# Cross-attention and FFN layer: the first batch's input transposes and first queries are issued ahead of the branch, and the start is reordered

## The reference

```python
def reference(...):                       # cut to what is computed
    q = layernorm(x) @ w_q;  k = ctx @ w_k;  v = ctx @ w_v          # 16 heads of 64
    attn = softmax(where(mask, -inf, q @ k.T / 8))
    x = x + (attn @ v) @ w_o
    w = int4_quantize(kernel)             # scale = max|kernel| / 7, round, clip, times scale
    h = layernorm(x)
    return x + h @ w + bias + (h @ a) @ b
```

## Time and profile before

| what | value |
|---|---|
| median of 3 runs | 540.42 us (539.54 to 540.65) |
| the profiled execution: time, span | 538.71 us, 536.9 us |
| mean granted TensorE clock in it | 0.958 |
| busy: PE, PEld, DVE, ACT, POOL | 468.2, 337.9, 423.2, 330.9, 400.3 us |
| busy in the first 30 us: PE, DVE, ACT, POOL | 7.30, 20.84, 17.29, 9.31 us |

### The profile page before, as it was taken

One profiled execution on the slowest core, in us unless ns is written; L12 is line 12 of the kernel. 1 busy time (PEld: TensorE's weight loads), 2 busy tenths in 40 slices (PEclk: granted clock), 3 DMA queues, 4 the chain that ended last, 5 costly groups with the idle time before them and its releaser, 6 DMA issues.

```text
span 536.9 us, 15609 instructions
## 1 busy us (share of the span) xinstructions
PE 468.2 (87%) x5939; PEld 337.9 (63%) x5939; DVE 423.2 (79%) x1138; ACT 330.9 (62%) x839; POOL 400.3 (75%) x658
## 2 busy tenths in 40 slices
PE   2239678998999899999999899989999999988874
PEld 0125365667766686667766776668666777666663
DVE  4945757988898888988898879888798878888762
ACT  4815456676667776676567666776667656666521
POOL 3364187888878787879878887878787787789941
PEclk9559979999999999999999999999999999999897
DMA  8310157668866788688767896688757786679950
GB/s 304 109 59 21 29 132 146 112 127 165 159 120 123 135 186 123 125 149 165 141 112 136 160 160 123 125 129 189 130 120 149 97 146 130 131 130 168 178 130 24
DMA packets 217953, 71.10 MB, mean 132 GB/s; under 512 B 202497, under 2 KB 216594, under 8 KB 217874
## 3 DMA queue, kind: packets, MB, share of 16 engines
q1 hardware_dynamic: 216528, 67.65, 64.9%
q0 software_dynamic: 768, 2.10, 1.2%
q10 hardware_dynamic: 578, 0.30, 0.2%
HBM read 15.50 MB, written 4.19 MB: 37 GB/s over the span
## 4 chain that ended last, share of the span: by engine, by line
PE 48%; DVE 27%; ACT 13%; POOL 5%; issue 4%; DMA 2%; POOLq 0%; DVEq 0%; ACTq 0%
PE ps_b L812 38%; DVE ps_a L703 6%; PE ps_a L874 6%; ACT arena L586 6%; DVE arena L696 4%; ACT arena L577 2%; PE ps_b L915 2%; DVE arena L652 2%; PE ps_b L891 2%; DVE arena L775 1%; DVE arena L707 1%; POOL arena L512 1%; DMA mask_u<-in_mask_1x1xSxS_bk_dram 1%; POOL arena L516 1%; ACT arena L593 1%
## 5 line engine op out<-in xcount | busy, mean ns | idle before, releaser
L812 PE MATMUL ps_b<-arena 128*128 128x65 f16 (+3 forms) x3456 | 346.3, 253 | 14.6 <-DVE arena L676 5.3
L812 PEld LDWEIGHTS ps_b<-arena 128*128 128x128 f16 x3456 | 234.2, 99 | 103.1 <-DVE arena L676 6.7
L586 ACT ACTIVATE arena<-ps_a,arena 128x160 f32<-128x160 f32 x512 | 159.4, 395 | 95.9 <-DVE arena L707 87.5
L516 POOL TENSOR_TENSOR arena<-arena 128x512 f16<-128x512 f32 x128 | 148.2, 1158 | 0.0
L512 POOL CAST arena<-arena 128x512 f16<-128x512 f32 x128 | 78.2, 611 | 74.7 <-ACT arena L586 74.7
L703 DVE TENSOR_REDUCE ps_a<-ps_a 128x4 f32<-128x640 f32 x128 | 105.4, 823 | 0.2
L874 PE MATMUL ps_a<-arena 64*128 64x160 f16 x1536 | 76.4, 233 | 14.5 <-ACT arena L586 11.2
L874 PEld LDWEIGHTS ps_a<-arena 64*128 64x128 f16 x1536 | 50.9, 95 | 39.2 <-issue 22.2
L891 PE MATMUL ps_b<-arena 128*128 128x65 f16 x512 | 71.7, 194 | 0.0
L696 DVE TENSOR_TENSOR arena<-ps_b,arena 128x512 f16<-128x512 f32 x64 | 43.7, 686 | 24.9 <-ACT arena L577 24.1
L775 DVE TENSOR_TENSOR arena<-ps_b,arena 128x256 f32<-128x256 f32 x128 | 54.3, 425 | 4.4
(11 more groups left out here) (122 smaller groups left out, 437.5 us busy)
## 6 DMA issues: line engine op xcount, KB each, us to landing
arena<-in_x_dram SPq DMA_DIRECT2D x8, 512.0 KB, 5.2
mask_u<-in_x_dram SPq DMA_DIRECT2D x32, 128.0 KB, 2.9
out_dram<-mask_u SPq DMA_DIRECT2D x32, 128.0 KB, 2.4
arena<-arena SPq DMA_TRANSPOSE x128, 3.8
arena<-in_L_xattn_w_k_dram SPq DMA_DIRECT2D x1, 1024.0 KB, 8.5
arena<-in_L_xattn_w_v_dram SPq DMA_DIRECT2D x1, 1024.0 KB, 10.5
arena<-in_L_xattn_w_q_dram SPq DMA_DIRECT2D x1, 1024.0 KB, 12.3
arena<-in_L_xattn_w_o_dram SPq DMA_DIRECT2D x1, 1024.0 KB, 14.2
```

What stands on the lines that cost most here:

```text
L516: nc.gpsimd.tensor_tensor(lo_main, main, hi_main, ALU.subtract)
L586: ins = nc.scalar.activation(probs[k % 2][:, h, :], p_scores[k % 2][:, h % 2, h // 2 * WINDOW:(h // 2 + 1) * WINDOW], ACT.Exp, bias=neg_ma ...
L812: mm = nc.tensor.matmul(dst, a, c, start=(first and at == 0), stop=(last and at == n - 1))
```

## The change

Names and order change; no instruction of the computation is dropped, and none is added except that some are issued at another place or in another form.

- The queries' weights are loaded and halved first (`W_ORDER`). POOL makes their low half ahead of the branch; that of the values moves behind it.
- Ahead of the branch TensorE also turns `xn` (`x0`, `x1`) and makes `q0`, `q1`, `q2`; ACT takes their high halves between its weight copies; DVE makes the low halves of `x0`, `x1` in the midst of its span chain. The low halves of `q0` to `q2` stand first behind the branch.
- The keys' scaled copy on ACT is gone: DVE makes the keys' low half in one instruction with the scaling (`scalar_tensor_tensor`) ahead of `q3`.
- The item order behind the branch is `q3 q4 q5 c q6 k0 k1 q7 k2 k3 v0 v1 r0 r1`. `maxima(0)` and `exps(0)` follow `k1`, the statistics follow `q7`, `keep` follows `k3`, `norm_apply` follows `v0`.
- The FFN weights are made in two parts, `ffn_grid` after `v0` and the rest after `r1`. The bias copy goes ahead of the branch, and the waits for FFN weights and output weights go to the first items that use them.

```diff
-        ALL_PROJ = [i for slot in PROJ for i in slot]
+        EARLY = ["x0", "x1", "q0", "q1", "q2"]
+        ALL_PROJ = EARLY + ["q3", "q4", "q5", "c", "q6", "k0", "k1", "q7", "k2", "k3", "v0", "v1", "r0", "r1"]
...
-        W_ORDER = (1, 2, 0, 3)
+        W_ORDER = (0, 1, 2, 3)
+        SCALED_ORDER = (0, 2, 3)
...
-            split_low(nc.gpsimd, 0)
+            split_low(nc.gpsimd, 2)
...
-            split_low(nc.vector, 1)
             for i, name in enumerate(ALL_PROJ):
+                if name in EARLY[0:DT]:
+                    continue
+                if name == "q3":
+                    dve.wait_ge(split_hi, 2)
+                    nc.vector.scalar_tensor_tensor(out=w_lo[1], in0=raw_w[1], scalar=WS, in1=w_hi[1], op0=ALU.mult,
+                                                   op1=ALU.subtract).then_inc(split_lo[1], 1)
                 item(start, i, name)
-                if name == "k3":
+                if name == "q7":
                     for t in range(ST):
                         norm_stats(t, 32)
                     norm_var()
-                if name == "q2":
+                if name == "v0":
+                    ffn_grid(dve)
+                if name == "k3":
...
-                if name == "q5":
+                if name == "k1":
                     maxima(0)
-                if name == "q7":
-                    ffn_weights(dve)
+            ffn_weights(dve)
...
-                if name == "q5":
+                if name == "k1":
                     scores(0)
-            pe.wait_ge(ffn_made, 1)
-            scores(1)
+                if name == "k2":
+                    pe.wait_ge(bias_copied, 1)
+                    scores(1)
             pe.wait_ge(keep_made, 1)
-            pe.wait_ge(split_lo[3], 1)
-            pe.wait_ge(ffn_split, 1)
...
-            split_low(nc.gpsimd, 2)
+            split_low(nc.gpsimd, 0)
             path(pool, fast_pool, general_pool)
...
+            high(0)
+            rescale(0)
+            for j in range(DT):
+                act.wait_ge(item_made, j + 1)
+                nc.scalar.activation(xT_hi[:, j, :], p_item[j][:, :], ACT.Copy).then_inc(item_hi, 1)
+            high(1)
+            high(2)
+            rescale(2)
+            for j in range(len(EARLY) - DT):
+                act.wait_ge(item_made, DT + j + 1)
+                nc.scalar.activation(f_q[0][:, 0, j, :], p_item[(DT + j) % LANES][:, :], ACT.Copy).then_inc(item_hi, 1)
+            high(3)
+            rescale(3)
             path(act, fast_act, general_act)
...
+            for j in range(DT):
+                dve.wait_ge(item_hi, j + 1)
+                nc.vector.tensor_tensor(xT_lo[:, j, :], p_item[j][:, :], xT_hi[:, j, :], ALU.subtract) \
+                    .then_inc(item_done, 1)
             link(nc.vector.tensor_tensor_reduce(out=scratch, in0=penalty, in1=key_left, scale=1.0, scalar=LOWEST,
                                                 op0=ALU.add, op1=ALU.max, accum_out=col(FIRST)))
...
+            dve.wait_ge(bias_made, 1)
+            nc.vector.tensor_copy(bias_all[:, :], p_bias[:, 0:D]).then_inc(bias_copied, 1)
             dve.wait_ge(ffn_max_spread, 1)
...
             nc.tensor.transpose(p_max_row, ffn_scale[:, 0:1], ident[:, :]).then_inc(ffn_max_turned, 1)
+
+            w_q_hi, w_q_lo = (w[0].rearrange("p (t n) -> p t n", t=DT) for w in (w_hi, w_lo))
+            pe.wait_ge(xn_made, ST)
+            for j in range(DT):
+                for t in range(ST):
+                    mm = nc.tensor.transpose(p_item[j][:, t * P:(t + 1) * P], xn[:, t, j * P:(j + 1) * P], ident[:, :])
+                mm.then_inc(item_made, 1)
+
+            pe.wait_ge(split_lo[0], 1)
+            pe.wait_ge(item_done, DT)
+            for j in range(len(EARLY) - DT):
...
             pe.wait_ge(ffn_max_row, 1)
```

More of the change, by code:

```diff
@@ L147, in xattn_ffn @@
         f_raw = Layout()
-        raw_w = [f_raw.take([DT * HD]) for _ in range(4)]
+        raw_q = f_raw.take([DT * HD])
+        f_raw.at = f.at // 2
+        raw_k, raw_v = f_raw.take([DT * HD]), f_raw.take([DT * HD])
         w_hi = [f.take([DT * HD], fp16) for _ in range(4)]
@@ L180, in xattn_ffn @@
         inv_sum = [f.take([GROUP]) for _ in range(2)]
+        f_raw.at = f.at
+        raw_w = [raw_q, raw_k, raw_v, f_raw.take([DT * HD])]
         attn = [f.take([HD]) for _ in range(2)]
@@ L412, in bank, with ffn_grid @@
                 return i % LANES
-        W_ORDER = (1, 2, 0, 3)
+        W_ORDER = (0, 1, 2, 3)
+        SCALED_ORDER = (0, 2, 3)
         def split_low(eng, i):
-            eng.wait_ge(scaled, W_ORDER.index(i) + 1)
+            eng.wait_ge(scaled, SCALED_ORDER.index(i) + 1)
             eng.tensor_tensor(w_lo[i], raw_w[i], w_hi[i], ALU.subtract).then_inc(split_lo[i], 1)
-        def ffn_weights(dve):
-            steps = [0]
+        ffn_link = [0]
+        def ffn_grid(dve):
+            ffn_link[0] = 0
             def link(ins):
-                steps[0] += 1
+                ffn_link[0] += 1
                 ins.then_inc(ffn_steps, 1)
-                dve.wait_ge(ffn_steps, steps[0])
+                dve.wait_ge(ffn_steps, ffn_link[0])
             dve.wait_ge(ffn_max_all, 1)
@@ L435, in ffn_weights, with link @@
             link(nc.vector.tensor_scalar(ffn_t[:, :, :], ffn_w[:, :, :], ffn_scale[:, 3:4], ROUND, ALU.mult, ALU.add))
+        def ffn_weights(dve):
+            def link(ins):
+                ffn_link[0] += 1
+                ins.then_inc(ffn_steps, 1)
+                dve.wait_ge(ffn_steps, ffn_link[0])
             link(nc.vector.tensor_scalar(ffn_w[:, :, :], ffn_t[:, :, :], ROUND, QMAX, ALU.subtract, ALU.min))
@@ L538, in slot @@
                 if s.u == 1 and s.norm_ahead:
-                    pool.wait_ge(item_made, 1 if s.batch == 0 else items_at[s.k - 1 - NS] + 1)
+                    pool.wait_ge(item_made, ALL_PROJ.index("c") + 1 if s.batch == 0 else items_at[s.k - 1 - NS] + 1)
                     gather(s.batch + 2)
@@ L857, in queries_done @@
                 if batch == 0:
-                    return ALL_PROJ.index(last) + 1
+                    return max(ALL_PROJ.index(last), ALL_PROJ.index(f"k{grp}")) + 1
                 u = next(u for u in range(NS) if last in PROJ[u])
@@ L925, in tail_item @@
                 else:
+                    if tile == 0:
+                        pe.wait_ge(ffn_split, 1)
                     pe.wait_ge(item_done, items_at[s.k - 1])
@@ L949, in after_setup @@
                 eng.wait_ge(raw_loaded[i], 16)
-            eng.wait_ge(scaled, 4)
+            eng.wait_ge(split_hi, 4)
+            eng.wait_ge(scaled, len(SCALED_ORDER))
             eng.wait_ge(split_lo[0], 1)
-            eng.wait_ge(split_lo[2], 1)
+            eng.wait_ge(item_hi, len(EARLY))
             eng.wait_ge(ffn_made, 1)
@@ L1264, in _, with high, rescale @@
                 nc.scalar.activation(mask_h[:, t, :], mask_u8[:, t, :], ACT.Copy).then_inc(mask_cast, 1)
-            for n, i in enumerate(W_ORDER):
+            def high(i):
                 act.wait_ge(raw_loaded[i], 16)
                 nc.scalar.activation(w_hi[i], raw_w[i], ACT.Copy, scale=WS).then_inc(split_hi, 1)
-                act.wait_ge(split_hi, n + 1)
+            def rescale(i):
+                act.wait_ge(split_hi, W_ORDER.index(i) + 1)
                 nc.scalar.activation(raw_w[i], raw_w[i], ACT.Copy, scale=WS).then_inc(scaled, 1)
+            high(0)
[11 more added lines that the diff above has]
+            rescale(3)
             path(act, fast_act, general_act)
@@ L1385, in _ @@
             nc.tensor.transpose(p_max_row, ffn_scale[:, 0:1], ident[:, :]).then_inc(ffn_max_turned, 1)
+            w_q_hi, w_q_lo = (w[0].rearrange("p (t n) -> p t n", t=DT) for w in (w_hi, w_lo))
[7 more added lines that the diff above has]
+            for j in range(len(EARLY) - DT):
+                cols = slice(j * P, (j + 1) * P)
+                for d in range(DT):
+                    for i, (w, x_half) in enumerate(((w_q_hi, xT_hi), (w_q_hi, xT_lo), (w_q_lo, xT_hi))):
+                        mm = nc.tensor.matmul(p_item[(DT + j) % LANES][:, :], w[:, d, cols], x_half[:, d, :],
+                                              start=(d == 0 and i == 0), stop=(d == DT - 1 and i == 2))
+                mm.then_inc(item_made, 1)
             pe.wait_ge(ffn_max_row, 1)
```

24 lines of the change are left out of this document (15 added, 9 removed).

## The result

533.65 us median (533.22 to 535.14, 4 runs) against 539.98: ratio 0.9899, 95% interval 0.9861 to 0.9937. The ratio is taken from the single runs and is not the quotient of the two medians, which differ by 6.3 and 2.7 us; by the ratios the change is faster by 5.5 and by 3.5 us. The intervals overlap, so the two measurements need not differ in anything but chance. The spread of the eleven runs, 5.8 us, is no sign of its own either: 33 of the 34 runs of the kernel before beside them lie between 536.34 and 544.16 (the last took 790.31). What two profiles of the changed kernel show is the main finding. Ratios are to the kernel before in the same call; e0 to e3, e4 to e7 and e10 to e13 are three calls, so across them ratios are compared and not times.

A forecast was written before the change was run, and what follows sets the result against it. No engine idles long (TensorE 87% busy) and the loop is fixed, so an earlier start shifts everything: 538.71 - 4.2 + 0.4 = 534.9 us profiled, 540.42 - 3.8 = 536.6 median; range 534.2 to 540.2.

The forecast's parts named there:

- Part 1: Ahead of the branch: DVE's chain loses 5.3 us, gets 2.2 back, and ends at 31.7 instead of 28.60.
- The two engines exclude each other: DVE's chain: L1335's 2.34 us was waiting for POOL's split; with POOL idle it costs about 0.16, saving 2.2.
- DVE waits for `x1`: Middle of DVE's chain: DVE stands still until `x1`'s low half is done at 21.95, so L1319 begins 5.3 us later.
- catch L1309: Rival, ahead of the branch: POOL's split begins before L1309, DVE stands until 18.2, 3.9 us later, no change (540.5); chance 0.12.
- Part 2: Branch to first maxima: DVE out 2.77 us after the chain, `q3` to `q5` end at 41.7, `c` at 44.15, `maxima(0)` until 47.85.
- I take DVE first: At the keys' low half: DVE at 36.45 goes ahead of POOL's split, which then runs from 38.75 to 42.8.
- The rival: At the keys' low half POOL wins: the half ends at 42.8, `c` at 45.95, 1.8 us less gain, 538.4; chance 0.18.
- Part 3: From `exps(0)` to the loop: `r1` ends at 59.0, FFN steps at 60.65, low half and so `maxima(1)` at 62.1.
- Sum: `maxima(1)` at 62.1 for 66.33, 4.2 us less; with 0.4 charged for the clock, median 536.6.
- The clock charge of 0.4: Around the loop's start: TensorE's low-clock episode begins some slots earlier; charged 0.4 us, between nothing and 1.7.
- The sign against the clock rival: Profile row 78 to 80 us before the change: the grant rose as soon as TensorE was fully busy.
- the clock rival: TensorE's clock stays low into batch 0: three more low slots eat the 3.8 us, six give 544.4; chance 0.08.

The follow-up runs named there:

- e0: The changed kernel measured again, against the kernel before: 535.78 us (11 runs), ratio 0.9935; GpSimd was first at the keys' low half in its profile.
- e3: Changed kernel with the FFN weights made in one piece behind `q7` and the statistics again: 535.34 us, ratio 0.993 to the kernel before.
- e4: Changed kernel with the last three FFN steps moved behind `maxima(1)`, their low half on DVE in slot 2: 533.88 us, ratio 0.9903 to the kernel before.
- e7: Changed kernel with fourteen unused matmuls of 512 columns behind `q2`: 532.7 us, ratio 0.9887 to the kernel before.
- e10: Changed kernel with GpSimd's low half of the values waiting for DVE's keys' low half, so DVE is always first: 532.96 us, ratio 0.988.
- e13: e12 plus e7's fourteen matmuls and ten more ahead of slot 1's `scores(3)`: 529.61 us, ratio 0.9831 to the kernel before.
- e6: Changed kernel with one more unused GpSimd subtraction of 128x1024 after `x1`'s low half, to meet DVE: 538.13 us, ratio 0.9979.
- e12: e10 with e4's move of the FFN steps, but their low half on GpSimd: 530.84 us, ratio 0.9848 to the kernel before.
- e5: Changed kernel with two more unused DVE instructions of 1024 columns in DVE's chain: 538.12 us, ratio 0.998; `maxima(1)` 2.59 us later than in e0.
- e11: Changed kernel with DVE's keys' low half waiting for GpSimd's low half of the values, so GpSimd is always first: 535.92 us, ratio 0.9937.
- the first profile: Profiled execution of the changed kernel's first measurement, DVE first at the keys' low half: 533.49 us.

## Why the prediction was right, point by point

**Part 1, right.** The two engines exclude each other, L1387 came to 0.16, L1363 was held and hidden; the chain's end was forecast at 31.7 and is 31.0 to 31.7 in the profiles of the changed kernel. e6 makes the same kind of collision on purpose. That DVE waits for `x1` was right too. GpSimd did not catch L1309 (L1357 now) in any profile, but the lead is small: 0.27 us in the first, 0.07 in e12's. That each us of DVE's wait counts in full is e5's result at `maxima(1)`.

**Part 2, right in kind, two terms off.** DVE came out of the branch 2.13 to 2.34 after the chain and not 2.77, and `q3` to `q5` took 5.4, not 6.5. Both shorten the quick schedule: `c`'s low half ended at 41.36 instead of 44.15, which is 2.1 us less behind the chain's end and 0.7 from the chain. "I take DVE first" is the step that failed in its form: it was treated as a fact about the kernel that I didn't know, with 0.18 for the other case, while two executions of the kernel came out differently. The rival's mechanism was exact (in it L732 was to end at 42.8 and `c` at 45.95; 42.63 and 45.54 in e0). Its price of 1.8 was too small, 3.0 by e10's and e11's times, because it was worked out against a `c` for which TensorE was ready late, at 41.7; with TensorE done at 39.3 nothing hides the wait. What the rival did not have at all is the second fall of the clock behind the wait, 1.2 us in e0 and e11.

**Part 3, right.** From the end of `c`'s low half to `maxima(1)` the forecast had 18.0 us, the first profile 17.8 (19.05 in e0, with the second fall of the clock). The FFN steps lie bare on the path, as forecast, and e4 and e12 take them off it.

**Sum.** -4.2 was forecast for `maxima(1)`; measured -7.1 in the quick schedule and -1.7 in e0's slow one. 536.6 lies between the two kinds, so that the number was near the mixture by luck and not by insight. The result is at the fast edge of what was forecast: 533.65 is 0.55 under the range's lower end of 534.2 in us, while the ratio 0.9899 against the 540.42 that the forecast started from gives 535.0, inside it. The clock charge of 0.4 was not measured apart. From `maxima(1)` to the piece of the loop at 165.07 it was 98.74 us before, and it is 99.37 in the first profile, 99.00 in e0 and 98.50 in e10, so a cost of that size is neither shown nor excluded. The stretch at the low clock did get longer, from about 6.9 to 13.6 us. The sign against the clock rival was misread, as TensorE was fully busy from 76 to 78 before at 0.50 too, and the grant rose only within the next window. The rival did not come true even so: the grant was back at 2.4 GHz soon after 74, in slot 4, as this window of the profile after shows:

```profile
74.00:76.00 2.00, 2.00 (x42) 1.75 (x39) 1.25 (x4) 1.47 (x6) 0.68 (x2) 0.96 0.53 103
```

## What to carry to other kernels

When two engines want the same exclusive resource within a few tenths of a us, look for the schedule that the other winner gives, and put in the wait that fixes the better order: here one wait for a semaphore that is already there made the difference between 0.9937 (e11) and 0.988 (e10) in one call. When the runs of one kernel spread over as much as the effect, compare two profiles of it before explaining the mean, and place the difference: here part of it lay at the start, in the race, and part near the end, where nothing was changed. DVE work that reads two SBUF tensors is best placed where GpSimd is idle, or given to GpSimd, as e12 did with the FFN weights' low half.

## What was unexpected of the hardware

- DVE's recorded start is not the time at which it holds the ports: L732 "starts" 0.61 us ahead of GpSimd's split in e0 and loses. In the quick profile the low half before it (L714) ended at 35.04, 0.27 ahead of GpSimd's first memset; in e0 at 35.87, 0.06 ahead. The memset itself is not what holds DVE: in e10 it began 0.08 behind the low half's end and L733 still took 2.28, as GpSimd's split was made to wait. That leaves the split itself, though its recorded start in e0, 36.39, is 0.52 behind the end of DVE's L714. When exactly it takes the ports no run shows.
- A train of GpSimd instructions back to back doesn't let DVE in between: 4.62 us for a 0.69 us instruction in e4. One-column DVE steps with a single tensor input (0.15 us) ran beside GpSimd's split before.
- A 0.2 us difference in a one-column matmul, 0.38 or 0.58 by TensorE's clock, goes with the one or the other order in all seven profiles, and the order is worth 3 us of kernel time.
- A wait of one engine can cost a second time through TensorE's clock: idle for 3.07 us in e0 in front of `c`, TensorE then ran at 1.2 GHz from 44.5 to about 47.5, and the stretch to `maxima(1)` was 1.2 us longer. In e6, idle for 2.82 at the same place, the clock stayed up.
- A gather's issue on GpSimd is held too: 2.84 us instead of 0.97 for L504 in e0, while DVE ran L732.
